# A layer of cross-attention and mixture of experts on one core: an output ahead of weight copies, three tiles' scores ahead of the values, the shared lower parts in odd steps

## What is computed

```python
def reference(x, ctx_1024, Wv, Wk, Wq, Wo, bo, router_w, router_b, w1, b1, w2, b2, sw1, sb1, sw2, sb2):
    x = x + xattn(ctx_1024, ctx_1024, layernorm(x))   # softmax(q k^T / 4) v per head, then Wo, bo
    z = layernorm(x)
    sh = gelu(einsum('nd,sdh->snh', z, sw1) + sb1)
    shared = (einsum('snh,shd->nd', sh, sw2) + sb2.sum(0)) / 2
    gates = z @ router_w + router_b                   # the two largest, and their softmax
    h = gelu(einsum('nd,edh->enh', z, w1) + b1)
    y = einsum('enh,ehd->end', h, w2) + b2
    return x + shared + einsum('ne,end->nd', comb, y)
```

## Time and profile before

| | |
|---|---|
| median of 3 runs | 349.05 us (346.09 to 352.2) |
| the profiled execution | 349.37 us |
| its span, first to last instruction | 347.7 us |
| PE busy, weight loads (PEld) | 313.0 us (90%), 273.2 us (79%) |
| DVE, ACT, POOL busy | 227.3 (65%), 216.8 (62%), 193.4 us (56%) |
| mean granted clock of PE | 0.972 |

### The profile page before, as it was taken

One profiled execution on the slowest core, in us unless ns is written; L12 is line 12 of the kernel. 1 busy time (PEld: TensorE's weight loads), 2 busy tenths in 40 slices (PEclk: granted clock), 3 DMA queues, 4 the chain that ended last, 5 costly groups with the idle time before them and its releaser, 6 DMA issues. The chain is left out here.

```text
span 347.7 us, 7628 instructions
## 1 busy us (share of the span) xinstructions
PE 313.0 (90%) x2366; PEld 273.2 (79%) x2366; DVE 227.3 (65%) x474; ACT 216.8 (62%) x437; POOL 193.4 (56%) x235
## 2 busy tenths in 40 slices
PE   3996998999689999998999999999699999999980
PEld 2764776676467878897898998999599999999980
DVE  0579897898943567787566455667557767666630
ACT  1253675876775786574556656677277777868640
POOL 5446899879893268776460000333456557456563
PEclk9996999999999999999899999999899999999996
DMA  7980000007100472346666523545436557534344
GB/s 248 407 333 2 1 2 1 2 0 270 35 16 3 141 268 79 137 139 178 183 221 182 132 111 105 91 69 93 61 54 86 92 79 109 83 38 50 46 45 45
DMA packets 27910, 36.85 MB, mean 106 GB/s; under 512 B 8384, under 2 KB 22080, under 8 KB 27488
## 3 DMA queue, kind: packets, MB, share of 16 engines
q1 hardware_dynamic: 19984, 25.02, 23.6%
q0 software_dynamic: 7456, 10.04, 17.1%
q10 hardware_dynamic: 432, 1.31, 1.1%
HBM read 23.17 MB, written 13.19 MB: 105 GB/s over the span
## 5 line engine op out<-in xcount | busy, mean ns | idle before, releaser
L508 POOL DMA_INDIRECT out<-xres,meta x39 | 65.1, 1669 | 43.0 <-DMA out<-xres,meta 21.4
L929 DVE TENSOR_TENSOR h_lo<-g,h_hi 128x512 fp32r<-128x512 f32 x32 | 23.3, 728 | 39.8 <-ACT g L633 36.5
L632 ACT ACTIVATE h_hi<-psS,sb1T 128x512 fp32r<-128x512 f32 x32 | 22.0, 688 | 34.5 <-PE psS L1215 30.4
L471 POOL TENSOR_TENSOR Pr<-Pr,inv 128x1024 f32<-128x1024 f32 x16 | 31.3, 1958 | 12.0 <-DVE inv L918 11.9
L718 ACT ACTIVATE s_hi<-psS,b1c 128x256 fp32r<-128x256 f32 x60 | 25.6, 490 | 19.6 <-PE psS L1260 19.6
L1276 PE MATMUL psP<-w_lo,s_hi 128*128 x120 | 30.2, 284 | 3.3 <-DVE xres L982 3.3
L1026 DVE TENSOR_TENSOR s_lo<-sraw,s_hi 128x512 fp32r<-128x512 f32 x30 | 20.6, 688 | 18.7 <-ACT sraw L721 14.8
L1276 PE MATMUL psP<-w_hi,s_hi 128*128 x120 | 30.1, 282 | 0.0
L1215 PE MATMUL psS<-xt_hi,s_lo 128*128 128x512 f32 x64 | 25.9, 405 | 0.0
L721 ACT ACTIVATE sraw<-psS,b1c 128x256 f32<-128x256 f32 x60 | 25.9, 503 | 0.0
L1215 PE MATMUL psS<-xt_lo,s_hi 128*128 128x512 f32 x64 | 25.7, 402 | 0.0
(11 more groups left out here) (238 smaller groups left out, 1013.8 us busy)
## 6 DMA issues: line engine op xcount, KB each, us to landing
wraw<-in_w SPq DMA_DIRECT2D x16, 512.0 KB, 5.1
xg<-xg_d SPq DMA_DIRECT2D x15, 256.0 KB
sraw<-in_sw SPq DMA_DIRECT2D x2, 1024.0 KB, 11.3
out<-xres SPq DMA_DIRECT2D x4, 512.0 KB
xres<-in_x SPq DMA_DIRECT2D x3, 512.0 KB, 9.3
xTs<-in_xT SPq DMA_DIRECT2D x3, 512.0 KB, 10.0
xg<-xg_d SPq DMA_DIRECT2D x9, 128.0 KB
xg_d<-filler SPq DMA_DIRECT2D x8, 130.0 KB
```

The source lines that it names most:

```text
L471: pool.tensor_tensor(out=Pr[:, t % NPR], in0=Pr[:, t % NPR], in1=inv[:, t % 2].unsqueeze(2).to_broadcast([P, NH, L]), op=ALU.mult).then_in ...
L508: pool.indirect_dma_start(out, bass.IndirectOffsetOnAxis(ap=meta[:, n, 0:1].bitcast(U32), axis=0), y[:, n % NYB], None, compute_op=ALU.add ...
L632: A.activation(h_hi[:, n % 2], h_bank[n % 2], ACT.Gelu, bias=bias).then_inc(hhi_done, 1)
L929: V.tensor_tensor(out=h_lo[:, n % 2], in0=g[:, n % 2], in1=h_hi[:, n % 2].bitcast(F32), op=ALU.subtract).then_inc(hlo_done, 1)
```

## The change

Seven edits. (1) `weighted(8)`, the last single tile's, stands at the end of step 9, ahead of the weight copies of the second pair, where it stood in step 10. (2) `output(q)` comes in step `8q+8`, ahead of that step's lower part, where it came in step `8q+9`. (3) PE makes `queries(0)` in two halves of 128 tokens in two banks, and scores 0, 1 and 2 with `queries(1)` ahead of the values. (4) The values are made from `ctxT` as two halves of 64 rows each; `ctx2`, its load and its semaphore are gone. (5) The statistics of tiles 4 to 15 are spread over steps 0 to 8 (1, 2, 2, 2, then 1 each), the aggregates stand behind the sum of the exponentials, and `rstd1` and `add_bias` follow. (6) The eight `shared_low` pieces come in steps 5, 7, 9, 11, 13, 15, 17 and 18, and PE waits for them piece by piece. (7) `WoT` is loaded after the second batch.

```diff
@@ steps of the statistics @@
+        stats_at = [TPB, TPB + 1, TPB + 3, TPB + 5, TPB + 7] + list(range(TPB + 8, NT + 1))
+        def stats_of(s):
+            return range(*stats_at[s:s + 2]) if s + 1 < len(stats_at) else ()
@@ sync @@
-            sp.dma_start(WoT[:], WoT_in).then_inc(ld_wo, 16)
             for b in range(1, B):
+                if b == 2:
+                    sp.dma_start(WoT[:], WoT_in).then_inc(ld_wo, 16)
@@ gpsimd @@
-            bias_at = [0, 4, 7, 9, 11, 13, 15, NT]
+            bias_at = [0, 4] + stats_at[1:]
+            low_at = [5, 7, 9, 11, 13, 15, NT + 1, NT + 2]
-                if s in (1, 3, 5):
-                    rstd1(s // 2 + 1)
+                if s in (3, 5, 9):
+                    rstd1((s + 3) // 4)
-                if 5 <= s < 5 + NSH * PPE:
-                    shared_low(s - 5)
+                if s in low_at:
+                    shared_low(low_at.index(s))
@@ scalar @@
-            A.dma_start(ctx2[:], ctx2_in).then_inc(ld_ctx2, 16)
-            queries(0)
+            for u, (bank, ready, done) in enumerate(((psD, q0_psum, q0_sb), (psA, qt_psum, qt_sb))):
+                act.wait_ge(ready, 1)
+                A.activation(QT[:, 0, :, u * P:(u + 1) * P], bank[:, 0:D].rearrange("p (f n) -> p f n", f=C), ACT.Copy).then_inc(done, 1)
@@ vector @@
-                if s < B - 1:
-                    for t in range(TPB * (s + 1), TPB * (s + 2)):
-                        stats(t)
-                    for t in range(TPB * (s + 1), TPB * (s + 2)):
-                        aggregate(t)
+                for t in stats_of(s):
+                    stats(t)
                 if 4 <= s < NT + 4:
                     t = s - 4
                     dve.wait_ge(att_psum, t + 1)
...
                     V.reduce_sum(sm[:, (s - 1) % 2], Pr[:, (s - 1) % NPR], axis=AX.X).then_inc(sum_done, 1)
+                for t in stats_of(s):
+                    aggregate(t)
                 n = s - FIRST_CHUNK
-                if CPG < n < CHUNKS and n % CPG == 1:
+                if 0 < n < CHUNKS and n % CPG == 0:
                     output(n // CPG - 1)
...
-                if 2 <= t < SINGLES + 2:
+                if 2 <= t < SINGLES + 1:
                     weighted(t - 2)
...
                 if i == 0:
+                    weighted(SINGLES - 1)
                     for k in range(2):
                         pair_weights(1, k)
@@ tensor @@
             pe.wait_ge(wq_done, 1)
-            queries(0)
+            pe.wait_ge(ld_xT[0], 16)
+            for u, (bank, ready) in enumerate(((psD, q0_psum), (psA, qt_psum))):
+                for f in range(C):
+                    for c in range(C):
+                        last = T.matmul(bank[:, f * P:(f + 1) * P], WqT[:, c, f * P:(f + 1) * P], xTs[:, c, u * P:(u + 1) * P],
+                                        start=(c == 0), stop=(c == C - 1))
+                last.then_inc(ready, 1)
             scores(0)
+            scores(1)
+            queries(1)
+            scores(2)
 
             pe.wait_ge(ld_wv, 16)
-            pe.wait_ge(ld_ctx2, 16)
             for i, bank in enumerate((psA[:, :], psP[:, 1])):
                 for b in range(2 * i, 2 * i + 2):
                     for c in range(C):
-                        last = T.matmul(bank[:, b % 2 * D:(b % 2 + 1) * D], ctx2[:, c, b].rearrange("p a k -> p (a k)"), WvT[:, c],
-                                        start=(c == 0), stop=(c == C - 1))
+                        for j in range(2):
+                            last = T.matmul(bank[j * L:(j + 1) * L, b % 2 * D:(b % 2 + 1) * D], ctxT[:, c, b * L:(b + 1) * L], WvT[:, c],
+                                            start=(c == 0), stop=(c == C - 1))
                 last.then_inc(v_psum, 1)
-            queries(1)
@@ shared_out @@
+                if m < CPG:
+                    pe.wait_ge(s_lo_done, PPE * e + 3 + k // 2)
@@ PE's loop @@
-                if s + 1 < NT:
+                if 2 <= s < NT - 1:
                     scores(s + 1)
...
                     if n == 0:
                         pe.wait_ge(shift_done, NT - 1)
-                        pe.wait_ge(s_lo_done, NSH * PPE)
+                    if n < CPG and k == 0:
+                        pe.wait_ge(s_lo_done, PPE * e + 2)
```

More of the change, by code:

```diff
@@ L123, in sem @@
             return es.enter_context(nc.semaphore(name))
-        (WkT, WvT, ctxT, ctx2, Wq, WqT, xTs, sb2_bc, Kbd, Vbd, QT, Pr, PT, OT, WoT, bo_bc, rows, x2T, routing) = over
+        (WkT, WvT, ctxT, Wq, WqT, xTs, sb2_bc, Kbd, Vbd, QT, Pr, PT, OT, WoT, bo_bc, rows, x2T, routing) = over
         sb("xres_rest", [P, NT * D - NXB * D])
@@ L1062, in scores @@
                 b = t // TPB
-                pe.wait_ge(qt_sb, t // 2 + 1)
+                if t == 0:
+                    pe.wait_ge(q0_sb, 1)
+                else:
+                    pe.wait_ge(qt_sb, t // 2 + 1)
                 if b == 0:
@@ L1382, in build @@
             WkT, WvT, ctxT = lay("WkT", [P, C, D]), lay("WvT", [P, C, D]), lay("ctxT", [P, C, B * L])
-            ctx2, Wq, WqT = lay("ctx2", [P, C, B, 2, L]), lay("Wq", [P, C, D]), lay("WqT", [P, C, D])
-            fit(2 * WPE, WkT, WvT, ctxT, ctx2, Wq, WqT)
+            Wq, WqT = lay("Wq", [P, C, D]), lay("WqT", [P, C, D])
+            fit(2 * WPE, WkT, WvT, ctxT, Wq, WqT)
             Kbd, Vbd, QT = lay("Kbd", [P, C, B, HPR, L]), lay("Vbd", [P, B, D]), lay("QT", [P, 2, C, QT_TOK])
@@ L1391, in build @@
             rows, x2T, routing = (rows_a, rows_b), (x2T_a, x2T_b), routing_a + routing_b
-            over = (WkT, WvT, ctxT, ctx2, Wq, WqT, xTs, sb2_bc, Kbd, Vbd, QT, Pr, PT, OT, WoT, bo_bc, rows, x2T, routing)
+            over = (WkT, WvT, ctxT, Wq, WqT, xTs, sb2_bc, Kbd, Vbd, QT, Pr, PT, OT, WoT, bo_bc, rows, x2T, routing)
         w_hi = sb("w_hi", [P, NE, WPE], F32R)
@@ L1425 @@
     X, F = "L0_xattn_", "L0_ffn_"
-    ctxT = rows_first(v["ctx_1024"].reshape(B * L, D).T)
     laid = {
```

11 lines of the change are left out of this document (5 added, 6 removed).

## The result

Before: 348.61 us median of 20 runs (346.05 to 356.03). After: 343.44 us median of 20 runs (339.32 to 346.69). The ratio is 0.9856, with a 95% interval of 0.9825 to 0.9887: 5.0 us less, where 8.1 were forecast. The profiled execution took 342.78, its span 341.1 where it was 347.7, so 6.6 less. Medians here count all executions; ratios, and the 5.0, compare only those in the faster of two states that the chip shows.

What follows compares the result with a forecast made beforehand. TensorE (PE), busy 90% of the span, was taken as the bound, so its halts and slow stretches counted. Gains 4.9 + 2.9 + 0.3 + 0 = 8.1 took the profiled 349.37 to 341.3, in the runs 341.0 us; range 337.5 to 346.5.

Steps and rivals of the forecast that it cites:

- part 2: Shared chunks: output(q) earlier on VectorE removes PE's halt at chunk 16 and slow step, 2.9, plus 0.29 at chunk 24.
- the opening: Start to tile 0's transposes: first scores earlier, but values later, transposes 0.4 sooner to 0.3 later, so nothing gained.
- Part 1: Passage to pairs: weighted(8) ahead of the weight copies removes PE's 3.29 halt and slow stretch, 4.9 gained.
- so 1.8 go with it: Behind chunk 16's halt: the slow step of 4.59 against a normal 2.82 vanishes with the halt, 1.8 gained.
- the 1.1 of halt ahead of it: Ahead of chunk 16's output: PE's 1.67 halt for output(1) goes, though 0.3 to 0.7 of it come back.
- rival (a): Chunk 16's halt comes from outside, not VectorE's order; output(q) gives only 0.3, total 343.9; chance 0.17.
- Parts 3 and 4: Opening and attention steps, with GpSimd's lower parts moved: together 0, between -3 and +4.
- puts up to as much in the way at 13 and at 15: Attention steps: GpSimd's moved lower parts remove the 1.36 halt but delay steps 13 and 15 by up to that.
- The 1.36: PE's wait for GpSimd at step 7 of the attention, expected to go when GpSimd's lower parts move.
- Rival (c): Tile 0 is 0.5 earlier, GpSimd halts go, nothing returns at 13 and 15: 3 more, 338.0; chance 0.12.
- (b): Opening: the values' halves don't share the array, 3.8 more; the gain shrinks to 4, total 345.0; chance 0.15.
- (d): Pairs: GpSimd's scatter-adds become the bound, kernel slower, 350 at 6.38 a pair, 351.6 at 6.5; chance 0.06.

Runs made afterwards that it cites:

- experiment 2: Changed kernel with output(q) back at its old place on VectorE, one chunk later; 337.90 us, ratio 0.9793 to the kernel before.
- experiment 10: Changed kernel with the 12 statistics of x back in VectorE's steps 0 to 2, four in each; 337.29 us, ratio 0.9771.
- experiments 8 and 11: Against the changed kernel: exp(0) and exp(1) ahead of the value copies, 337.64 us (0.9672); values ahead of queries(1) and scores(2), 335.95 us (0.9742).
- Experiments 7: Changed kernel with output(0) back behind chunk 9's work, output(1) and output(2) still early; 337.81 us, ratio 0.9762.

## Why the prediction was right, and where it wasn't

The total lies in the range, 2.4 above the forecast, and 1.4% below the kernel before, short of the 2% at which the prediction drew its line (faster had 0.55, the same 0.39). That the total came so close is in good part luck: part 2 and the opening were both wrong, and in the profiled execution the two errors, 6.1 too little and 4.6 too much gain, nearly cancel.

**Part 1 was right in each step.** 4.9 were forecast, 5.07 came (16.18 less 11.11). `weighted(8)` starts directly behind the lower part, the copies come in time, `pair_hidden(1)` takes 2.87. Undone, it costs 5.4 in the medians. GpSimd's chain caught up in the profiled execution, but not in the two or three pairs that I gave it: its first pair goes out at 255.82, and only the eleventh waits for its rows for over a microsecond (1.20, at 310.34).

**Part 2 failed, in the step "so 1.8 go with it" and in the 1.1 of halt ahead of it.** I read the halt at chunk 16 as VectorE's order, since PE started again 0.16 behind VectorE's first bank. It did wait for that bank; but `output(1)` came 1.37 later than the same order brings it in experiment 2 (2.65 against 1.28 behind hidden part 17), because ScalarE's high parts of chunks 15 and 16 were late by 1.34 and 0.86 against the 1.58 of an undisturbed trace, and VectorE's own 0.43 came on top. I had looked only at the 0.43. No trace of the kernel before is free of such idle times, so its undisturbed halt, 0.30, is read from experiment 2's. By the runs the order is worth 0.64 for `output(1)` and 0.65 for `output(2)` (0.29 forecast). `output(0)`, counted at nothing, costs 0.7 to 0.8: the table that PE wants is made by `one_hot`, which now has output(0) and what that pushed back ahead of it, and PE had no slack there, it waited 0.43 already. Together 0.5 instead of 2.9 + 0.3. The step was wrong in cause: rival (a), 0.17, had it right that most of the halt came from outside. It did not see that such idle times would fall in the new kernel's runs too, which is what makes 2.9 of loss in the profiled execution.

**Parts 3 and 4, counted at 0, gave 4.6 in the profile, some 1.5 of it chance.** (i) The start was 1.5 earlier in that execution: 0.64 because the keys' product began sooner, its weights' load being there, and 0.86 because that product took 2.71 instead of 3.57. (ii) The first queries in halves: 0.70 to 1.1, forecast 0.6, and I let it vanish behind exp(0). My sum put exp(0) 10.6 to 11.3 behind the first scores, with products of 1.9 to 2.3 a bank; they take 1.95 and 1.90, and it is 10.12. From the first scores to tile 0's transposes it is 14.84, and my sum made it 15.3 to 16.0 (28.5 to 29.2 less 13.2); before it was 15.12. The Trainium skill, "TensorE: Matmul & The Clock Gate", under "Why this matters for your kernels", says that small products whose weights have fewer than 128 columns run at once where their outputs start in different partition groups; the trace agrees, 16 records of 64 columns take the 1.90 to 1.95 that eight of 128 take (1.89 to 1.99). (iii) GpSimd's odd steps, the step that failed: "puts up to as much in the way at 13 and at 15" was wrong. The 1.36 went and 0.05 came back, 0.95 in the undone run. (iv) The spread statistics, which I took to be free at best: tile 1's transposes come 19.25 behind the first scores, where they came 20.44 and 20.45 in the two traces of before, in the second of which PE stood waiting there for 1.11 us for GpSimd, its granted clock back at 1.00, so the clock isn't the cause. By experiment 10 this is worth 0.4 at chunk 0. (v) PE's clock made 0.3 of the difference between the two traces of before (84.92 and 84.60 from the first scores to chunk 0), no more. From 84.60 to 82.57 it is 2.0, of which 0.3 at tile 0, 0.95 and 0.4 are accounted for; some 0.4 stay open.

Rival (c) described this part and gave it 0.12; its lines for step 7 and for 13 and 15 are what the rows show, and tile 0 is 0.3 earlier counted from the first scores and 1.0 from the first queries, where it said 0.5.

**The rivals (b) and (d).** (b) is out by the rows of the values. (d) did not occur in the kernel after, but experiments 8 and 11 show its mechanism at work in single executions, at 1.6 to 1.8 us. Moving VectorE's copies did nothing to the issue of a scatter-add: 1562 ns as a rule and 2072 at most, against the earlier trace rows.

Without ScalarE's idle times the stretches add up to 5.1 (part 1) + 0.5 (part 2) + 0.7 (first scores) + 2.0 (from there to chunk 0) = 8.3 us, and kernels like the changed one are 8.1 to 8.4 under the kernel before on the chip where no trace has such times (336.78 of 344.92, 337.29 of 345.68). This is next to the forecast's 8.1, made of other parts. The 5.0 of the twenty runs would be these less what the idle times of ScalarE take from the new kernel beyond what they take from the old. That the two kernels differ in how much they lose to them is what two traces each suggest (1.7 and 0.8 for before, 5.2 and 2.4 for after, from chunk 11 to 18, against 20.48 and 19.84 where ScalarE doesn't stand still). Experiments 7 and 8, in the new order, have 0.6 and 2.8. So it is not shown, and neither is what the idle times come from.

## What to carry to other kernels

Ahead of pricing a halt as one engine's order, read the idle times of all engines at that place: if another stands still with nothing to wait for, the halt may be that execution's, and the slow stretch behind it too; a second trace of the same kernel tells. Price a moved step also by what stands behind its new place, and look how long that is wanted. Where an opening is bound by a copy ahead of the first activation, change the order on that engine; giving the matmul engine more work ahead of what the copy needs makes it later. And before a slow stretch is counted as a cost, look whether the engine had a wait behind it that takes it up.
